# Where the scan of a state-space layer reads its input in three of sixteen steps: GpSimd's product in SBUF itself, or ScalarE's copy of it in PSUM

## The reference

```
dA = exp(dt_t[:, :, None] * A)
h  = dA * h + dt_t[:, :, None] * B_t[:, None, :] * u_t[:, :, None]
y  = einsum('bds,bs->bd', h, C_t)
```

## Time and profile before

| | us |
|---|---|
| time, median of 3 runs | 2651.08 (2651.05 to 2653.18) |
| the profiled execution's own time | 2652.19 |
| its span, from first to last instruction | 2650.4 |
| the iterations 0 to 12, with given steps | about 80 to 796 |
| the iterations 13 to 31 | about 796 to 2071 |
| dense and routed experts | the rest |

### The profile page before, as it was taken

One profiled execution on the slowest core, in us unless ns is written; L12 is line 12 of the kernel. 1 busy time (PEld: TensorE's weight loads), 2 busy tenths in 40 slices (PEclk: granted clock), 3 DMA queues, 4 the chain that ended last, 5 costly groups with the idle time before them and its releaser, 6 DMA issues. The chain is left out here.

```text
span 2650.4 us, 22739 instructions
## 1 busy us (share of the span) xinstructions
PE 2367.8 (89%) x6064; PEld 1052.7 (40%) x6064; DVE 2057.3 (78%) x2025; ACT 1563.2 (59%) x2433; POOL 2047.8 (77%) x1269
## 2 busy tenths in 40 slices
PE   6688988889888999999999999999998899999586
PEld 4233333333333333333343333333333344444364
DVE  4899999999999999988998999899989443333221
ACT  4676777777775667666666666666666233222132
POOL 4699999999997799988899888888889432321276
PEclk9799999999999999999999999999999999999798
DMA  7565455644556766666666666566666500100254
GB/s 232 191 212 204 157 181 203 215 170 142 173 184 215 245 230 232 232 222 215 222 235 222 214 224 226 207 219 226 224 231 205 179 21 9 36 10 9 65 113 64
DMA packets 216892, 464.88 MB, mean 175 GB/s; under 512 B 29436, under 2 KB 109122, under 8 KB 216770
## 3 DMA queue, kind: packets, MB, share of 16 engines
q1 hardware_dynamic: 204786, 455.30, 51.0%
q0 software_dynamic: 11264, 7.98, 1.9%
q10 hardware_dynamic: 720, 0.23, 0.0%
HBM read 440.00 MB, written 23.99 MB: 175 GB/s over the span
## 5 line engine op out<-in xcount | busy, mean ns | idle before, releaser
L893 DVE TENSOR_TENSOR_SCAN hh<-decays,psdB 128x1024 f32<-128x1024 f32 x512 | 1165.6, 2283 | 53.4 <-ACT decays L715 20.0
L1030 POOL TENSOR_TENSOR products<-hh,Clo 128x1024 f32<-128x1024 f32 x408 | 961.5, 2360 | 153.7 <-DVE hh L893 150.9
L454 PE MATMUL psY<-products,ident 128*128 128x512 f32 x1708 | 820.1, 604 | 90.2 <-POOL products L1030 54.9
L715 ACT ACTIVATE decays<-dt,Acur 128x508 f32<-128x508 f32 x1024 | 668.0, 708 | 5.9 <-DVE hh L893 5.5
L882 DVE TENSOR_TENSOR psdB<-psT,Blo 128x1024 f32<-128x1024 f32 x395 | 484.1, 1226 | 65.7 <-ACT psT L683 32.6
L454 PEld LDWEIGHTS psY<-products,ident 128*128 128x128 f32 x1708 | 320.3, 193 | 525.8 <-issue 369.4
L1458 DVE TENSOR_TENSOR ac<-sg,d_bank 128x512 f32<-128x512 f32 x135 | 92.8, 688 | 225.4 <-PE d_bank L1308 175.6
L434 PE MATMUL psW<-xnT,wcur 128*128 128x512 f32 x496 | 227.2, 600 | 34.9 <-ACT u L646 18.9
L1030 POOL TENSOR_TENSOR products<-hh,late 128x1024 f32<-128x1024 f32 x104 | 244.1, 2367 | 11.7 <-PE psY L454 11.7
L728 ACT ACTIVATE late<-psdB 128x512 f32<-128x512 f32 x153 | 90.6, 592 | 233.0 <-PE psT L502 177.8
L1034 POOL TENSOR_TENSOR products<-products 128x512 f32<-128x512 f32 x170 | 215.6, 1268 | 13.3
(11 more groups left out here) (215 smaller groups left out, 3035.2 us busy)
## 6 DMA issues: line engine op xcount, KB each, us to landing
Blo<-rows SPq DMA_DIRECT2D x280, 512.0 KB, 6.0
Clo<-rows SPq DMA_DIRECT2D x280, 512.0 KB, 5.2
late<-rows SPq DMA_DIRECT2D x104, 512.0 KB, 6.5
wcur<-taps_l SPq DMA_DIRECT2D x31, 512.0 KB
fw<-in_Wg SPq DMA_DIRECT2D x36, 256.0 KB, 5.6
fw<-in_Wu SPq DMA_DIRECT2D x36, 256.0 KB, 4.5
fw<-in_Wd SPq DMA_DIRECT2D x36, 256.0 KB, 5.1
disp<-fw SPq DMA_DIRECT2D x16, 528.0 KB, 7.8
```

What stands on the lines that cost most here:

```text
L454: ins = pe.matmul(psY[:, :], lhsT=ident[:, :], rhs=gg[k % NGB][:, j, :], start=False, stop=(k % NK == NK - 1 and j == last - 1))
L715: ins = act.activation(dA[k % NDA][:, j, :, 1:T], dt[i % 2][:, c, :, 1:T], ACT.Exp, scale=Acur[i % 2][:, s:s + 1])
L893: dve.tensor_tensor_scan(out=hh[k % NHB][:, :, :].rearrange("p c t -> p (c t)"), data0=dA[k % NDA][:, :, :, :].rearrange("p c q t -> p (c ...
L1030: ins = pool.tensor_tensor(gg[k % NGB][:, :, :], hh[k % NHB][:, :, :], tile(Clo, Chi, slot(i, s)), ALU.mult)
```

## The change

At the given steps the scan reads POOL's product where it lies, in SBUF. ACT's copy, with its semaphore moved, is gone. What waited for the copy now waits for others: the scan for gave; POOL, before it overwrites one of the two given buffers, for the scan that read it; SP, before it first loads expert weights over those buffers, for the last scan that reads one.

```diff
@@ load_gate (SP)
-                        sp.wait_ge(moved, helped(NSTEP * NIT))
+                        sp.wait_ge(scan, given_steps[-1] + 1)
@@ ScalarE
-                def move_given(i, k):
-                    n = NSTEP * i + k
-                    act.wait_ge(gave, helped(n) + 1)
-                    at_least(act, scan, n + 1 - NDB)
-                    act.activation(dB[k % NDB][:, :, :], given[helped(n) % 2], ACT.Copy).then_inc(moved, 1)
...
-                        if k > 0 and assisted(i, k - 1):
-                            move_given(i, k - 1)
@@ scan_step (VectorE)
                     if assisted(i, k):
-                        dve.wait_ge(moved, helped(n) + 1)
+                        dve.wait_ge(gave, helped(n) + 1)
...
-                                           data1=dB[b][:, :, :].rearrange("p c t -> p (c t)"), initial=0.0, op0=ALU.mult, op1=ALU.add).then_inc(scan, 1)
+                                           data1=(given[helped(n) % 2] if assisted(i, k) else dB[b][:, :, :]).rearrange("p c t -> p (c t)"), initial=0.0, op0=ALU.mult, op1=ALU.add).then_inc(scan, 1)
@@ give (GpSimd)
-                    at_least(pool, moved, helped(n) - 1)
+                    if helped(n) > 1:
+                        pool.wait_ge(scan, given_steps[helped(n) - 2] + 1)
```

More of the change, by code:

```diff
@@ L190, in wave_phase @@
         names = ("wcur_ld wready wfree dbu da scan prod half red stat moments rs1 rs2 rstd_ok centred skipped par_ok kept_ok exp_ok ln_ok dt_ok dtu_ok placed silu_ok "
-                 "ycopied ygated gave moved cleared zero zeroed x_ld x1_ok x_st gated gfree sg_ok scaled upped acted downed sum_ok").split()
+                 "ycopied ygated gave cleared zero zeroed x_ld x1_ok x_st gated gfree sg_ok scaled upped acted downed sum_ok").split()
         (wcur_ld, wready, wfree, dbu, da, scan, prod, half, red, stat, moments, rs1, rs2, rstd_ok, centred, skipped, par_ok, kept_ok, exp_ok, ln_ok, dt_ok, dtu_ok, placed, silu_ok,
-         ycopied, ygated, gave, moved, cleared, zero, zeroed, x_ld, x1_ok, x_st, gated, gfree, sg_ok, scaled, upped, acted, downed, sum_ok) = (sem(n) for n in names)
+         ycopied, ygated, gave, cleared, zero, zeroed, x_ld, x1_ok, x_st, gated, gfree, sg_ok, scaled, upped, acted, downed, sum_ok) = (sem(n) for n in names)
         ids_ld, raw_ld, cw_ld, wo_ld, par_ld, moe_ld, cst, tapped, saved = (sem(n) for n in "ids_ld raw_ld cw_ld wo_ld par_ld moe_ld cst tapped saved".split())
@@ L221, in helped @@
             return sum(assisted(a // NSTEP, a % NSTEP) for a in range(n))
+        given_steps = [n for n in range(NSTEP * NIT) if assisted(n // NSTEP, n % NSTEP)]
         def made(n):
```

## The result

The changed kernel takes 2769.05 us (median of 4 runs, 2757.12 to 2774.35) against 2651.22 for the kernel before: a ratio of 1.0443, 95% interval 1.0422 to 1.0464. It is slower, as forecast, but by 118 us and not by 55, and 33 us beyond the range. The runs also differ among themselves by 17 us; those of the kernel before differ by 2 here and by 13 among the 19 that ran beside e1 to e4. The profiled execution took 2771.0 us, its span 2769.2.

The account below looks back on a forecast made before the run. POOL, nearly full, was to bound the kernel: 53.05 + 3 x 1.95 = 58.9 us an iteration, 12 x 4.4 = 52.8, plus 3.9 in iteration 0, less 1 and 1, 55 us more: 2706 us, range 2676 to 2736.

Parts of the forecast that it names:

- what bounds the kernel: Stage with given steps: POOL and DVE nearly full, 52.9 and 52.0 of 54.5 us an iteration; POOL's slack 1.45 us.
- what is removed: ACT's 39 copies of 1.02 us, 39.8 us in all; removing them gains 1 us, once, in iteration 0.
- the price of a turn: At each given scan, POOL's next operation waits for the scan: POOL loses 2.26 - 0.19 - 0.12 = 1.95 us.
- two rows of much shorter instructions: Adapter stage, DVE beside POOL's products: the second to start was late by 0.24 of 0.43 us overlap, or 0.08 of 0.20.
- The split into a front and an end: POOL's product does not read for 0.12 us at its front and 0.19 at its end, so a scan costs less.
- the prediction's sum: Should each scan block POOL for its whole 2.26 us, the sum would be 67 us in place of 57.
- what POOL then makes of the iteration: POOL per iteration with three given scans: 53.05 + 3 x 1.95 = 58.9 us, 4.4 more.
- The scan starves: Rival: the scan waits until POOL runs out of products; 9.7 us an iteration, 126 in all, about 2775 us; 7 in 100.
- the wait at step 7: DVE's 1.38 us wait for ACT's decays at step 7, expected to cover the 1.4 us scan wait at step 4.
- the DVE instruction at 52.72: Adapter stage: DVE got its turn at the end of POOL's running product, another queued 0.03 us after; evidence against starving.
- PE's clock: Longer PE idling may add stretches at 1.2 GHz, perhaps 1 us each, lifting the forecast to 2715 us or so.
- the 38 long POOL operations: Sign of being right: one POOL operation near 4.3 us (2.36 + 1.95) at each given scan, 38 in all.

Follow-up runs that it names:

- e1: Changed kernel with ACT's copy and its wait kept, though the scan still reads POOL's product in SBUF and nobody reads the copy: 2772.9 us, 1.045.
- e4: Changed kernel with ACT writing the decays of the given steps into PSUM, so the scan's only SBUF input is POOL's product: 2649.72 us, 0.9998.
- e2: Changed kernel, but the given scans read the old contents of the PSUM buffer, not POOL's product, so one SBUF input each: 2650.62 us, 0.9997.
- e7: Changed kernel, but only scans of step 9 read POOL's product in SBUF; steps 4 and 13 keep ACT's copy: 2679.8 us, second group 2679.71.
- e10: Changed kernel, with POOL writing one column of zeros, without a wait, ahead of its products of steps 2, 3 and 11: 2705.82 us, 1.0211.
- e5: Changed kernel, with POOL waiting for the end of its own operation ahead of its products of steps 2, 3 and 11: 2706.2 us, 1.0209.
- e6: Changed kernel, but only scans of step 13 read POOL's product in SBUF; steps 4 and 9 keep ACT's copy: 2762.82 us, 1.0423.
- e9: Changed kernel, with POOL's dtu and gate moved from steps 11 and 12 to behind its product of step 13: 2766.27 us, 1.0449.

## Why the prediction was wrong

**Right: what bounds the kernel and what is removed.** The copies were to be worth 1 us at most, the moved waits nothing. e2 has both changes, the copies gone and the waits moved, and takes 2650.62 us; e1 puts the copy back and is as slow as the kernel after.

**Right: two inputs from SBUF, and the price of a turn.** The scan itself stays at 2.265 us (step 9, e7). e4 shows that it is the second SBUF input that matters. POOL was to lose 1.95 us for each scan, worked out from two rows of much shorter instructions and called the weakest step; it lost 1.89 (step 9) and 1.99 (step 4), so the size held, and that it is less than the whole scan. The split into a front and an end fits only roughly: the scan came in 0.12 us before the recorded end of POOL's operation, where 0.19 was taken. The Trainium skill (SBUF — State Buffer, § SBUF: two separate sides) says that whoever starts first has the shared ports for its whole instruction, and the other is blocked. The trace agrees in kind, and by 1.9 of 2.27 us. (With the whole 2.26 us the prediction's sum comes to 68.5 us, not the 67 that it gives.)

**Right: what POOL then makes of the iteration.** 58.9 us, if each scan has its turn. e10 has 58.8 and e5 59.0, and their times, 2705.8 and 2706.2, are the forecast's 2706 us. The sum for an iteration holds where the scan gets its turn. That the total agrees to 1 us is in part luck: from the starts of the scans, iteration 0 cost 4.3 us (e5) and 4.5 (e10) where 2.9 was forecast, and the later iterations made up 3.6 and 2.4 where 1 was.

**Wrong: when the scan gets its turn.** The step that failed is: "a given scan, 2.26 us, finds a POOL product under way, waits for its rest, and then POOL's next operation waits for the scan". At step 9 the scan was the first to start, and at step 4 it went as said in ten of the 12 iterations in which it had to wait. At step 13 the scan waited through four more operations in ten of 13 iterations: 9.1 us for DVE in place of the 1.3 given for it. So DVE, which was to stay shorter than POOL, became the bound: 53.1 + 0.6 + 9.1 + 1.8 = 64.6 us an iteration in place of 58.9.

The rival "The scan starves" named this mechanism and came to about 2775 us, close to the 2769. Its parts were off both ways: 6.3 us at step 13 (measured 9.1: it counted the running product, dtu and one product more, but the scan came while dt was still running, so that the product of step 11 counted in full, and the gate as well) and 2.4 each at steps 4 and 9 (measured 0.6 and 0); and it took off 1.4 for the wait at step 7, which did not go away but grew to 1.8. So its total came out close by errors that cancel. It got 7 in 100 on one piece of evidence, the DVE instruction at 52.72 that came in at the end of POOL's running product. That is one seam between two operations, and it was taken for the rule. That POOL's operations follow each other without a gap was in the rival's own text; it deserved more weight than one row of another stage.

**Not separated: PE's clock.** The forecast held it for a lift of some us in its range, and in e5 and e10, at 0.92 and 0.94, the iteration came out at its 59 us without a lift. In the kernel after PE idles up to 3.2 us in one piece at the turn shown, the granted clock is at 0.50 there, x0 takes 5.18 us, and the wait for the decays of step 7 is 1.8 us in place of gone; but ACT's 9.47 us behind the late scan delays the same chain. In e6 the wait is 2.4, and it made that experiment's time miss what was expected. No run changes the clock by itself.

**Signs named ahead.** "Scans over 4.5 us or a POOL that idles next to a waiting scan (starving)": both are in the trace, 11.36 us and the idle of 2.22. The iteration of 59 us and the 38 long POOL operations are not; POOL's long ones stand at steps 4 and 9 and at the three turns of step 13.

**What stays open.** Why a scan is passed over at one seam and let in at the next. At the same seam, dt to the product of step 11, it was let in three times and passed over ten times in the kernel after, and let in 11 times of 13 in e9, where only later operations had been moved. The overlap of the two POOL records does not tell the cases apart: 0.05 us where it was let in, 0.03 to 0.07 where it was passed over. With a pause of 0.08 us or an operation that reads nothing the scan was let in at 25 places of 25 each (steps 4 and 13 of e5 and e10); what decides without them is not known. Since e9 let it in at 23 places of 25 with neither, a part of what e5 and e10 gained may come from what else shifted in them.

## What to carry to other kernels

A DVE instruction with two SBUF inputs next to a GpSimd that works without pauses may wait not for one operation but for GpSimd's whole queue, here 9.1 us for a scan of 2.26; ask what GpSimd has queued when the instruction starts, and bound the wait by all of it. Keep one of the inputs in PSUM, even if another engine must copy it there, as long as that engine has time: the copy cost nothing here (e2, e4). If both must lie in SBUF, an operation of 0.1 us on GpSimd that reads nothing, put where the scan is due, went with a loss of 57 us in place of 118 here.

## What the runs showed of the hardware that had not been expected

- **Back-to-back POOL operations mostly keep the scan out, and the first seam decides.** In the kernel after, where POOL's next operation was recorded as starting 0.03 to 0.08 us before the end of the one under way, the waiting scan was passed over at 44 such seams (ten times four at step 13, twice two at step 4) and let in at 13, always the first after it had started to wait, and never at a later one. The traces of all the kernels say the same: at the first seam without a gap the scan was let in 84 times and passed over 52 times, at later ones it was let in at none of 92, and then it waited until POOL had nothing ready.
- **Where 0.08 us passed without POOL** (e5), the scan came in at 25 places of 25, and at 25 of 25 where an operation of 0.10 us that reads nothing stood, with no pause at all (e10). Without either it ranged from one in 13 (e6) to 23 in 25 (e9).
- **The scan's turn begins before the recorded end of POOL's operation**, by 0.12 us (647.44 against 647.56 at the gate of iteration 8). That is part of why a turn costs POOL 1.9 us and not 2.26.
- **Which seams let the scan in differs from run to run** (three short scans at step 13 in the kernel after's profiled execution, in iterations 2 to 4; two in e1's, in 1 and 12), each worth 4 to 6 us (iterations of 58.2 to 60.9 us in place of 64.7). It may be a part of the 17 us between the kernel's fastest and slowest run, but that is not shown: the kernel before spreads by 13 us in 19 runs, and the two runs of e7's second group, in which the scan is always first, by 12.
